# Cross-attention block: denominators stored in pairs of slots, weight quarters in other slots, fewer weight transfers, V ahead of the joint projection in four slots

## The reference

```python
h = layernorm(x, ln1_g, ln1_b)
x = attention(h, h, sa_wq, sa_wk, sa_wv, sa_wo, sa_bo) + x
h = layernorm(x, ln2_g, ln2_b)
x = attention(h, ctx, ca_wq, ca_wk, ca_wv, ca_wo, ca_bo) + x
h = layernorm(x, ln3_g, ln3_b)
p = h @ ff_w1 + ff_b1                       # 256 -> 2 x 1024
x = (p[..., :1024] * gelu(p[..., 1024:])) @ ff_w2 + ff_b2 + x
# attention: 16 heads of 64; softmax((q @ k.T) * 64 ** -0.5) @ v, then @ wo + bo
```

## Time and profile before

| | us |
|---|---|
| median of 3 runs | 1746.31 |
| lowest and highest | 1742.96, 1747.38 |
| the profiled execution | 1743.33 |
| its span, first to last instruction | 1741.5 |
| TensorE busy | 1701.8 (98%) |
| VectorE busy | 1406.2 (81%) |
| ScalarE busy | 1236.6 (71%) |
| GpSimd busy | 1086.2 (62%) |

### The profile page before, as it was taken

One profiled execution on the slowest core, in us unless ns is written; L12 is line 12 of the kernel. 1 busy time (PEld: TensorE's weight loads), 2 busy tenths in 40 slices (PEclk: granted clock), 3 DMA queues, 4 the chain that ended last, 5 costly groups with the idle time before them and its releaser, 6 DMA issues.

```text
span 1741.5 us, 39097 instructions
## 1 busy us (share of the span) xinstructions
PE 1701.8 (98%) x11712; PEld 1564.2 (90%) x11712; DVE 1406.2 (81%) x2964; ACT 1236.6 (71%) x3370; POOL 1086.2 (62%) x1812
## 2 busy tenths in 40 slices
PE   9999999999999999999999999999999999999999
PEld 8998898989999999889888899999999888888888
DVE  8897788888888888788888888888888877656664
ACT  7887777878888888778778788888888776222222
POOL 7775577767766666688777777777776555222211
PEclk9999999999999999999999999999999999999999
DMA  7775577778766677887777788776666776211210
GB/s 217 182 184 144 155 201 189 195 194 213 194 179 156 157 176 194 214 208 189 197 202 200 206 207 205 175 184 169 166 168 161 177 200 159 73 49 61 66 45 25
DMA packets 321234, 288.92 MB, mean 166 GB/s; under 512 B 104064, under 2 KB 281344, under 8 KB 321024
## 3 DMA queue, kind: packets, MB, share of 16 engines
q1 hardware_dynamic: 267232, 273.29, 60.4%
q10 hardware_dynamic: 53792, 13.12, 3.5%
HBM read 82.98 MB, written 37.49 MB: 69 GB/s over the span
## 4 chain that ended last, share of the span: by engine, by line
PE 64%; SPq 17%; issue 4%; DMA 4%; POOL 4%; DVE 3%; ACT 3%; ACTq 0%; POOLq 0%; DVEq 0%
PE QKB L526 9%; PE PVB L597 9%; PE PTB L539 8%; PE WOP L577 6%; PE VB L461 5%; PE PTB L1184 5%; PE S L1184 5%; SPq L632 5%; SPq L630 4%; PE S L428 4%; PE S L429 4%; SPq L1502 4%; PE QKB L1202 3%; PE VB L1202 3%; PE QKB L508 2%
## 5 line engine op out<-in xcount | busy, mean ns | idle before, releaser
L734 ACT ACTIVATE PT<-S,NM 128x256 f32<-128x256 f32 x1024 | 471.1, 472 | 193.2 <-DVE NM L862 192.5
L837 DVE TENSOR_TENSOR PL<-PTB,PH 128x512 fp32r<-128x512 f32 x512 | 350.8, 686 | 147.8 <-ACT PH L761 125.3
L1075 POOL TENSOR_TENSOR ON<-ON,RB 128x256 f32<-128x256 f32 x256 | 187.9, 734 | 283.9 <-DVE ON L882 261.4
L862 DVE TENSOR_REDUCE NM<-S 128x2 f32<-128x512 f32 x512 | 326.4, 679 | 0.4
L761 ACT ACTIVATE PH<-PTB 128x1024 fp32r<-128x1024 f32 x256 | 265.5, 1037 | 41.3 <-PE PTB L539 39.7
L539 PE MATMUL PTB<-IDN,PT 128*128 128x128 f32 x2048 | 271.3, 274 | 5.2 <-DVE PL L837 5.1
L428 PE MATMUL S<-RX 128*128 128x256 f32 x1012 | 254.9, 284 | 2.4 <-DMA RX<-QKS 1.9
L429 PE MATMUL S<-RX 128*128 128x256 f32 x1012 | 254.0, 283 | 0.0
L577 PEld LDWEIGHTS WOP<-WO,OT 128*128 128x128 f32 x1536 | 216.1, 190 | 38.7 <-POOL OT L1080 19.2
L526 PE MATMUL QKB<-HT,WA 128*128 128x512 f32 x936 | 242.4, 394 | 2.3 <-DVE QKS L843 2.0
L539 PEld LDWEIGHTS PTB<-IDN,PT 128*128 128x128 f32 x2048 | 230.0, 140 | 10.8 <-DVE PL L837 10.2
(11 more groups left out here) (151 smaller groups left out, 2941.9 us busy)
## 6 DMA issues: line engine op xcount, KB each, us to landing
RX<-QKS SPq DMA_DIRECT2D x506, 192.0 KB, 2.9
RX<-QKS SPq DMA_DIRECT2D x506, 128.0 KB, 2.9
RB<-denominators SPq DMA_DIRECT2D x512, 64.0 KB, 2.7
weights<-SPL SPq DMA_DIRECT2D x48, 256.0 KB, 3.3
out_dram<-XR SPq DMA_DIRECT2D x32, 256.0 KB, 3.7
WA<-weights SPq DMA_DIRECT2D x64, 128.0 KB, 2.7
rows<-XN SPq DMA_DIRECT2D x24, 256.0 KB, 2.6
rows<-HF SPq DMA_DIRECT2D x23, 256.0 KB, 2.7
```

What stands on the lines that cost most here:

```text
L734: last = e.activation(PT[:, c % 2, j * S:(j + 1) * S], S1[:, i, qt * S:(qt + 1) * S], ACT.Exp, bias=NM[:, j:j + 1], accum_out=DEN[:, c % 2 ...
L837: e.tensor_tensor(PL[:, cols], PTB[:, i, :], PH[:, s % 2, cols].bitcast(F32), ALU.subtract).then_inc(a.dve_pl, 1)
L862: e.tensor_reduce(NM[:, i * TT:(i + 1) * TT], S1[:, i, :].rearrange("p (t s) -> p t s", t=TT), AX.X, ALU.max, negate=True).then_inc(a.dve_ ...
```

## The change

1. Denominators in pairs. DEN, RDEN and the DRAM buffer hold the sums of two slots (8 columns). Reciprocal and small transpose run in odd slots alone. SP saves and broadcasts once for two slots, the broadcasts after the ring copies. RB is filled for both slots by the same two transfers, after the multiplication of the last slot of the pair before.
2. Weight quarters. `QUARTERS` is (3, 4, 5, 6) for the cross-attention weights. Those of the feed-forward part are split at pairs `HALVES` = (5, 6), two quarters per row of slots, over twice as many rows (slots 136 to 231); staging comes every second row. Stores count on one semaphore for each SPL buffer.
3. The scale 1/8 is taken out of the weights and multiplied once into gain and bias of the second layer norm (one activation on LNG in slot 16).
4. Weight transfers. `load_pair` moves four blocks in one issue instead of one block pair in each of two loops, `load_four` 512 columns instead of 256.
5. In slots 25 to 28 TensorE computes its part of V before the joint projection instead of after it.

The diff, cut:

```diff
-CROSS_LOADS = 4
+VALUE_LOADS = 2
-QUARTERS = (1, 2, 5, 6)
+QUARTERS = (3, 4, 5, 6)
+HALVES = (5, 6)
-        DEN = sb("DEN", [P, 2, 4])
+        DEN = sb("DEN", [P, 8])
@@ pe_slot
+            if late and joint(c + LEAD):
+                pe_value_turn(e, c)
             if joint(c + LEAD):
                 pe_project_both(e, c + LEAD)
             if alone(c + AHEAD) and not late:
                 pe_project(e, c + AHEAD)
-            if 0 <= c < ATT:
+            if 0 <= c < ATT and not (late and joint(c + LEAD)):
                 pe_value_turn(e, c)
@@ act_gain_bias
+            if n == B:
+                e.wait_ge(s_gain, 1)
@@ act_slot
-                sl.wait(e, a.dve_rc, c - 1)
+                sl.wait(e, a.dve_rc, c // 2)
@@ dve_slot
-            if sl.has(c):
+            if sl.has(c) and c % 2:
+                m = c // 2
                 sl.wait(e, a.act_exp, 2 * c + 2)
-                if c > 1:
-                    e.wait_ge(d_ds[(c - 2) % 4], 16 * ((c - 2) // 4 + 1))
-                e.reciprocal(RDEN[:, 0:4], DEN[:, c % 2, :]).then_inc(a.dve_rc, 1)
-                sl.wait(e, a.dve_rc, c + 1)
-                e.transpose(RDT[:, c % 2, :], RDEN[:, :]).then_inc(a.dve_rt, 1)
+                if m > 1:
+                    e.wait_ge(d_ds[(m - 2) % 4], 16 * ((m - 2) // 4 + 1))
+                e.reciprocal(RDEN[:, 0:8], DEN[:, :]).then_inc(a.dve_rc, 1)
+                e.wait_ge(a.dve_rc, m + 1)
+                e.transpose(RDT[:, m % 2, :], RDEN[:, :]).then_inc(a.dve_rt, 1)
@@ pool_split_w
             if k > 1:
-                e.wait_ge(d_ws, 16 * (k - 1))
-            if done == 0 and n < KD:
-                e.tensor_scalar(STG[:, cols], STG[:, cols], SCALE, None, ALU.mult).then_inc(s_sc, 1)
-                e.wait_ge(s_sc, k + 1)
+                e.wait_ge(d_ws[k % 2], 16 * (k // 2))
@@ pool_weights
-            if pair in QUARTERS and B + 1 <= seq <= B + NCH:
-                pool_split_w(e, seq - B - 1, 3 + NCH + seq - B, QUARTERS.index(pair), NCH)
+            if pair in HALVES and B + 1 <= seq <= B + 2 * NCH:
+                n, half = divmod(seq - B - 1, 2)
+                pool_split_w(e, n, 4 + NCH + n, 2 * half + HALVES.index(pair), NCH)
@@ pool_slot
-                e.wait_ge(d_rb[s % 2], 32 * (s // 2 + 1))
+                e.wait_ge(d_rb[s // 2 % 2], 32 * (s // 4 + 1))
@@ act_attention_slot
             if sl.c == PAIRS * 2:
                 e.wait_ge(d_sm, 16 * 5)
+                e.activation(LNG[:, 1, :, :], LNG[:, 1, :, :], ACT.Copy, scale=SCALE).then_inc(s_gain, 1)
@@ sync: save_den, spread_den
-            def spread_den(s):
-                e.wait_ge(d_ds[s % 4], 16 * (s // 4 + 1))
-                if s >= 2:
-                    e.wait_ge(a.pl_or, s - 1)
+            def spread_den(m):
+                e.wait_ge(d_ds[m % 4], 16 * (m // 4 + 1))
+                if m:
+                    e.wait_ge(a.pl_or, 2 * m)
                 else:
-                    e.wait_ge(s_ow, s + 1)
+                    e.wait_ge(s_ow, 2)
                 for i in range(2):
-                    e.dma_start(RB[OWN[i], s % 2, :],
-                                DS[s % 4, TT * i:TT * (i + 1), :].rearrange("t p -> (t p)").partition_broadcast(P // 2)) \
-                        .then_inc(d_rb[s % 2], 16)
+                    e.dma_start(RB[OWN[i], :, :],
+                                DS[m % 4, 0:8, :].rearrange("(x i t) p -> i x (t p)", i=2, t=TT)[i]
+                                .partition_broadcast(P // 2)).then_inc(d_rb[m % 2], 16)
@@ sync: loads
-            def load_pair(phase, p, *chunks):
-                for n in chunks:
-                    e.dma_start(WA[:, n, :, cols].bitcast(F32), WS[phase, :, n, :, cols]).then_inc(d_wq[p % 2], 16)
+            def load_pair(phase, p):
+                e.dma_start(WA[:, 0:4, :, cols].bitcast(F32), WS[phase, :, 0:4, :, cols]).then_inc(d_wq[p % 2], 16)
             def load_four(phase, g, n):
-                cols = slice((2 * g + n % 2) * QW, (2 * g + n % 2 + 1) * QW)
+                cols = slice(g * HC, (g + 1) * HC)
@@ sync: the loop
             for c in range(-AHEAD, ATT + 2):
-                if c >= 2:
-                    spread_den(c - 2)
...
-                if 1 <= c <= ATT:
-                    save_den(c - 1)
+                if 2 <= c <= ATT and c % 2 == 0:
+                    save_den(c // 2 - 1)
                 if 0 <= c - 1 + AHEAD < ATT and c - 1 >= -AHEAD:
                     k = c - 1 + AHEAD
                     if k >= DIRECT:
                         copy_ring(e, k)
+                if 2 <= c <= ATT and c % 2 == 0:
+                    spread_den(c // 2 - 1)
```

More of the change, by code:

```diff
@@ L286, in block_kernel @@
         d_wst = sem("d_wst")
-        d_ws = sem("d_ws")
+        d_ws = [sem(f"d_ws{n}") for n in range(2)]
         d_wq = [sem(f"d_wq{n}") for n in range(2)]
@@ L303, in block_kernel @@
         s_ph = sem("s_ph")
-        s_sc = sem("s_sc")
+        s_gain = sem("s_gain")
         s_pw = sem("s_pw")
@@ L734, in act_slot @@
                         last = e.activation(PT[:, c % 2, j * S:(j + 1) * S], S1[:, i, qt * S:(qt + 1) * S],
-                                            ACT.Exp, bias=NM[:, j:j + 1], accum_out=DEN[:, c % 2, j:j + 1])
+                                            ACT.Exp, bias=NM[:, j:j + 1],
+                                            accum_out=DEN[:, c % 2 * 4 + j:c % 2 * 4 + j + 1])
                     last.then_inc(a.act_exp, 1)
@@ L1538, in store_split, with await_stored @@
                 e.dma_start(WS[n // NCH, :, n % NCH, :, quarter * QW:(quarter + 1) * QW],
-                            SPL[:, k % 2, :, :].bitcast(F32)).then_inc(d_ws, 16)
-            def load_pair(phase, p, *chunks):
+                            SPL[:, k % 2, :, :].bitcast(F32)).then_inc(d_ws[k % 2], 16)
+            def await_stored(phase):
+                for done in d_ws:
+                    e.wait_ge(done, 16 * QTR // 2 * NCH * (phase + 1))
+            def load_pair(phase, p):
                 cols = slice(p * P, (p + 1) * P)
-                for n in chunks:
-                    e.dma_start(WA[:, n, :, cols].bitcast(F32), WS[phase, :, n, :, cols]).then_inc(d_wq[p % 2], 16)
+                e.dma_start(WA[:, 0:4, :, cols].bitcast(F32), WS[phase, :, 0:4, :, cols]).then_inc(d_wq[p % 2], 16)
             def load_four(phase, g, n):
-                cols = slice((2 * g + n % 2) * QW, (2 * g + n % 2 + 1) * QW)
-                e.dma_start(WA[:, 4 + n // 2, :, cols].bitcast(F32), WS[phase, :, 4 + n // 2, :, cols]) \
-                    .then_inc(d_wv[g], 16)
+                cols = slice(g * HC, (g + 1) * HC)
+                e.dma_start(WA[:, 4 + n, :, cols].bitcast(F32), WS[phase, :, 4 + n, :, cols]).then_inc(d_wv[g], 16)
             def fill_weights(c):
@@ L1557, in fill_weights @@
                     store_split(QTR * (seq - SPLIT) + QUARTERS.index(pair))
-                if pair in QUARTERS and B + 1 <= seq <= B + NCH:
-                    store_split(QTR * (NCH + seq - B - 1) + QUARTERS.index(pair))
+                if pair in HALVES and B + 1 <= seq <= B + 2 * NCH:
+                    store_split(QTR * NCH + 2 * (seq - B - 1) + HALVES.index(pair))
                 for phase, first in ((0, SLOTS), (1, ATT)):
@@ L1562, in fill_weights @@
                         g, i = divmod(p, QUAD)
[L1563 to L1573, removed]
-                                e.wait_ge(a.pe_qk, freed)
-                                if p > 1 and half == 0:
-                                    e.wait_ge(d_wq[p % 2], 16 * CROSS_LOADS * (PAIRS // 2 * phase + p // 2))
-                                load_pair(phase, p, 2 * half, 2 * half + 1)
+                        if phase and g:
+                            k = ATT - QUAD + i
+                            at = k
+                            freed = nth_alone(k) + 1
+                        else:
+                            j = first - 2 * PAIRS + 2 * p + 1
+                            at = j - LEAD + 3
+                            freed = nth_joint(j) + 1
+                        if c == at:
+                            await_stored(phase)
+                            e.wait_ge(a.pe_qk, freed)
+                            if p > 1:
+                                e.wait_ge(d_wq[p % 2], 16 * (PAIRS // 2 * phase + p // 2))
+                            load_pair(phase, p)
                     for g in range(2):
                         four = first - 2 * PAIRS + PAIRS * g + QUAD
-                        for n in range(4):
-                            if c == four + 2 + n:
-                                e.wait_ge(d_ws, 16 * QTR * NCH * (phase + 1))
+                        for n in range(2):
+                            if c == four + 2 + 2 * n:
+                                await_stored(phase)
                                 e.wait_ge(a.pe_v, tiles(four) + 2)
@@ L1619, in weights @@
                     stage_rows(ca_wo[half:, :])
-                if pair == 0 and B + 1 <= seq <= B + NCH:
```

(8 more changed lines are left out.)

20 lines of the change are left out of this document (10 added, 10 removed).

## The result

The changed kernel took **1718.82 us** (median of 4 runs, 1716.5 to 1719.94), the kernel before 1744.63 beside it (4 runs, 1742.15 to 1747.38): ratio 0.985, 95% interval 0.983 to 0.987, so 25.8 us less. The forecast was 1718.7 within 1709 to 1731, and 27.6 us less. The profiled execution of the changed kernel took 1719.03 us with a span of 1717.2, 24.3 less than before's 1741.5.

The account below looks back on a forecast made before the run. TensorE was taken as the bound, busy 1701.8 of 1741.5 us. Terms -20 - 5.3 - 3 + 0.7 = -27.6 us from the median 1746.31 gave 1718.7 us, range 1709 to 1731.

Parts of the forecast that it names:

- Quarters: Slots 32 to 80 and 136 to 184: splitting weight quarters in other slots gains 7.2 and 12.8 us, together 20.
- The SPL turnover: Quarter at pair 5 waits for the store of pair 3's: 0.8 us late, under a cover of 1.8, so 0.
- rival 2: SPL turnover stalls GpSimd at pair 5, so the quarters give 17 us only: 1722 to 1730 us; chance 0.10.
- Fewer issues on SP, passage: Slots 112 to 136: two slots' 20 SP issues become 13, gaining 5.3 of 6.2 us; bounds 3 and 6.2.
- Pairs, arithmetic: VectorE: 128 reciprocals and as many small transposes go, worth 0; bounds 0 and -1 us.
- V first: Slots 25 to 28: TensorE's idle time only moves behind the transposes, worth 0; bounds 0 and -2 us.
- Pairs, price: One RB buffer for both slots makes multiplications wait for broadcasts: +0.7 us; bounds 0 and 90.
- the prediction's own signs: Right: multiplication hardly ever waits for RB. Wrong: GpSimd waiting for broadcasts or for stores of SPL.
- it costs from a landing of 5.7 us up: Broadcasts into the single RB buffer cost time only when landing takes 5.7 us or more; longest seen 6.4.
- cover of 1.8: Output projection (WOP) starts after its OT split has ended, leaving 1.8 us in which a late split costs nothing.
- spare of 0.9: Cross slot: broadcasts land at 1127.5, the next multiplication starts at 1128.44, so 0.9 us to spare.
- The end: Last slots: fewer SP issues cut waits for landed ring copies, gaining 3 us; bounds 0 and -6.7.

Follow-up runs that it names:

- measured alone: Only the weight quarters in their new slots and the scale in the layer norm's gain, on the kernel before: 1724.34 us, ratio 0.9897.
- staging first: Kernel before with reciprocals, save and broadcasts once for two slots, and SP issuing the staging transfer ahead of the broadcasts; quarters unmoved: 1720.65 us, ratio 0.9874.
- the one with one and two extra issues: Changed kernel with small transfers ahead of each pair's broadcasts: one in slots 88 to 112 and 184 to 208, two in 208 to 232: 1724.39 us.
- pairs alone: Kernel before with reciprocals, save and broadcasts once for two slots and one semaphore per SPL buffer, nothing else: 1760.66 us, ratio 1.0105.
- loads alone: Kernel before with load_pair and load_four in fewer, larger issues, nothing else: 1733.09 us, ratio 0.9951.
- three extra issues: Changed kernel with small transfers ahead of each pair's broadcasts: three in slots 88 to 112 and 184 to 208, five in 208 to 232: 1768.04 us.
- one load moved: Changed kernel with one 512 KB weight load of the last phase moved from slot loop 248 to 250: 1713.59 us, run again 1713.10 us.

## Why the prediction was right, and where it was not

**Quarters: right in size and in the main cause.** Forecast -7.2 and -12.8, measured alone -7.6 and -13.3, in the whole -6.8 and -13.5. The subtraction of regular slots from loaded ones gave the size without needing the cause. For the cause the prediction gave the wait for staging and the collision with the bias add; staging first with the quarters unmoved, on top of the pairs, brought 4.2 and 11.8 of it, so the wait was the main part. The prediction did not see why the transfer was late: it stood on SP behind other issues.

**The SPL turnover: the wait of rival 2 is there, and pricing it at 0 was right.** GpSimd waits 18.0 us in 7 waits:

```profile
POOL SPL L1023 <- DMA weights<-SPL: 18.0, 7, 3.9
```

With the stores ahead of the broadcasts it fell to 3.1 us, and slots 32 to 80 took 267.24 instead of 268.03. But another run with the stores behind, the one with one and two extra issues, took 267.25 there. So the cover held for all but 0.8 us, and perhaps for all.

**Fewer issues on SP, passage: right.** Forecast -5.3 of 6.2, measured -5.8 in the whole, -5.1 by pairs alone, -6.8 by loads alone. Either part alone frees SP enough; the second adds nothing, one reason why the parts don't add. SP has idle time there, as forecast: its waits for other engines and for transfers add up to 31.6 us in the passage, and to 3.1 before. Late landings can take 3.6 us of the gain back, and cost 2 us or more in three of seven executions.

**Pairs, arithmetic: right**, 0: regular slots took 133.69 after and 133.67 before. V first: right, 0; and as forecast the idle time before the joint projection is gone, while it stands before the later one:

```profile
163.25 1.58 PE L527 MATMUL QKB<-HT,WA 128*128 128x512 f32 x6
167.20 0.98 PE L509 MATMUL QKB<-HT,WA 128*128 128x256 f32 x6 [0.78 <-DVE QKS L857]
```

**Pairs, price: a number that came near by luck, from a wrong working.** Forecast +0.7, one outlier of 6.4 us; in the profiled execution of the changed kernel the longest landing was 4.9 and the cost 0, in another program with the same broadcasts it was 8.0 and 3.6. Two of the prediction's own signs went against it: that the multiplication would hardly ever wait for RB was to show it right, and GpSimd waiting for broadcasts or for stores of SPL was to show it wrong. GpSimd waited 39.9 us for the one and 18.0 for the other. The time was right all the same, since TensorE waited only 0.3 us for OT: the signs named waits, not what they cost. The step that failed is "it costs from a landing of 5.7 us up". It added a cover of 1.8 to a spare of 0.9 for every pair, and the runs with extra issues show that a lasting delay costs from about the first 0.6 us. Had the median been 4.5 instead of 3.1, the forecast would have said 0. An estimate from the two and three extra issues (1.2 and 1.8 us of delay) says 0.3 to 0.8 us a pair, 41 to 102 us over 128 pairs if the self-attention slots behaved as the cross ones; they lost less, 0.45 a pair with three extra issues.

The Trainium skill, "DMA: Bandwidth & Descriptors", section "Latency and other measured facts", gives 2 us as HBM access latency at high load against 0.2 on average. The runs agree that late landings come with load, but a whole transfer can be later than that: the late broadcast, which reads DRAM, landed 4.9 us after its median. The late ring copy, 5.3 us after its median, goes from SBUF to SBUF, which is not what the page's figure is of.

**Pairs, what was missed: what stands behind the broadcasts.** The prediction said that they wait on SP "ahead of weight stores and the next ring copies", and did not count the staging transfer, which is behind them too. It was worth 40 us, the difference between pairs alone and pairs with staging first. The total did not suffer only because the change moves the quarters to pair 3 and later: at least two slots lie between transfer and use, and GpSimd's waits for staging are gone from the profile after. Without that move, or the staging issued first, the pairs lose. That the one part hid what the other would have cost was luck as far as the forecast goes.

**The end: wrong sign.** Forecast -3, measured +1.2. The step that failed is "bounds 0 and -6.7": it left no room for a loss. Fewer issues made SP earlier, and the transfers fell onto full DMA engines: a wait of 3.75 us in slot 249, which took 11.16 instead of 7.30. With one load moved the term is -3.2.

**The sum.** Forecast -27.6; measured -25.8 by the medians and -24.3 by the spans of the two profiled executions. The stretches add up to -24.5: -20.3 instead of -20, -5.8 instead of -5.3, +1.2 instead of -3, 0 instead of +0.7, and +0.4 in slots 184 to 232, which is within the spread (two executions with the load moved gave 260.85 and 261.33). That the forecast time of 1718.7 met the median of 1718.82 to 0.1 us is luck: the gain was 1.8 us smaller, and the kernel before, with one more run, came out 1.7 us lower. The one large error of size was the end, 4.2 us; an error that mattered far more was hidden by another part of the same change.

## What to carry to other kernels

When a wait moves on an in-order queue, list everything that is queued behind it in every slot, the rare transfers too, and issue ahead of it whatever doesn't need it: here the order of two calls was worth 40 us in one kernel. A spare that lies outside a closed loop (a consumer's cover) is used once, not once per turn; go around the loop and add up. And a queue that is freed issues earlier: look at the DMA share of the stretch, and spread large loads before claiming the gain.

## What the hardware showed unexpectedly

- Landing times have a long tail under load: 128 KB ring copies landed in 3.1 us at the median and 8.4 at the longest in a stretch with a DMA share of 1.08 at 244 GB/s (9.6 in another program's passage); one broadcast took 8.0 with a median of 3.1, and in another execution of the same program the longest was 5.3.
- What an issue costs SP does not follow its bytes: mostly 0.5 to 0.6 us, as 0.53 for 512 KB of weights, 0.59 for staging, 0.61 for each of the three small extra ones (1.82 in all), but also 0.39 for another 512 KB load. Two broadcasts of 128 KB each took 1.24 with the pairs, and 1.10 to 1.12 before at 64 KB each; the median to landing rose from 2.7 to 3.1 us. Single issues took far longer, up to 1.75 us for a broadcast of the changed kernel.
- After a wait of 3.75 us TensorE's granted clock was 0.60 and 0.54 over the next 4 us; it had been 1.00 in the 6 us window in which it was busy for 4.00. In the kernel before it was 0.50 from 856 to 858 us, shortly after a wait of only 2.04 us.
